# An attention-and-experts layer on one core: stacked operands copied through DRAM instead of within SBUF and by identity products

## The reference, cut to what matters

```
x = x + layernorm(attention(layernorm(x)))
x = x + layernorm(experts(layernorm(x)))

attention:  Q, K, V = x @ w_qkv;  Q_l, K_l = means of 16 tokens of Q, K
            kernel1 = softmax(Q K_l^T); kernel2 = softmax(Q_l K_l^T); kernel3 = softmax(Q_l K^T)
            out = (kernel1 @ iterative_inv(kernel2)) @ (kernel3 @ V) @ w_proj
experts:    loss_e = mean((relu(x Wd1_e) Wd2_e - x)^2);  e = argmin loss
            out = x W_base + relu(x Wa_down_e) Wa_up_e  (+ biases)
```

## Time and profile before

| | |
|---|---|
| median of three runs | 2256.9 us |
| the profiled execution | 2251.81 us |
| its span, first to last instruction | 2250.1 us |
| TensorE busy | 2045.9 us (91% of the span) |
| VectorE busy | 1471.5 us (65%) |
| ScalarE busy | 864.0 us (38%) |
| mean granted TensorE clock | 0.987 of full speed |

### The profile page before, as it was taken

The page is one execution under the profiler, slowest core; times in us unless marked ns, Lnnn a source line. Parts: engine busy times, 40 slices in busy tenths (PEclk is TensorE's granted clock), DMA queues, the critical chain, the costliest instruction groups (busy, mean ns, idle before and its releaser), DMA issues.

```text
span 2250.1 us, 59443 instructions
## 1 busy us (share of the span) xinstructions
PE 2045.9 (91%) x25341; PEld 1321.1 (59%) x25341; DVE 1471.5 (65%) x3319; ACT 864.0 (38%) x1509; POOL 701.1 (31%) x916
## 2 busy tenths in 40 slices
PE   4889999999999999999999999999999999999955
PEld 2655657566574756657475565756657475665724
DVE  4667575776757676675766767576675767767541
ACT  3334344343434434343344434334343443434221
POOL 4153142422315232332523224252231524223052
PEclk9999999999999999999999999999999999999978
DMA  6223151331414122151422315132231513213020
GB/s 156 45 54 71 30 130 33 90 63 42 102 30 124 38 80 65 20 133 30 116 47 70 64 30 132 30 100 53 64 80 30 131 32 88 64 35 92 12 57 19
DMA packets 232974, 150.74 MB, mean 67 GB/s; under 512 B 153035, under 2 KB 203732, under 8 KB 232693
## 3 DMA queue, kind: packets, MB, share of 16 engines
q1 hardware_dynamic: 232710, 146.95, 27.7%
HBM read 36.98 MB, written 16.78 MB: 24 GB/s over the span
## 4 chain that ended last, share of the span: by engine, by line
PE 60%; DVE 18%; SPq 8%; issue 4%; ACT 3%; POOL 3%; DMA 2%; DVEq 1%; POOLq 0%; ACTq 0%
PE NS L986 11%; PE ringF L1194 9%; SPq L429 8%; PE ringF L1179 6%; PE KV L1067 5%; PE ringA L1153 5%; PE ringA L880 4%; DVE mx L1541 3%; PE ringF L1227 3%; DVE stage L1631 3%; PE ringA L1053 3%; PE ringA L1029 3%; PE ringF L880 2%; PE ringF L1229 2%; ACT E L690 2%
## 5 line engine op out<-in xcount | busy, mean ns | idle before, releaser
L1194 PE MATMUL ringF<-x,H 128*128 128x256 f16 x1536 | 237.9, 273 | 0.0
L1555 DVE TENSOR_REDUCE mx<-ringA 128x8 f32<-128x512 f32 x256 | 175.6, 686 | 88.4 <-PE ringA L1029 87.9
L682 ACT ACTIVATE E<-ringA,score_scale 128x512 f32<-128x512 f32 x256 | 175.4, 686 | 116.3 <-PE ringA L1053 115.9
L1194 PE MATMUL ringF<-H 128*128 128x128 f16 x1024 | 204.5, 220 | 1.4 <-DVE H L1642 1.4
L1608 DVE SCALAR_TENSOR_TENSOR X<-X,NS 128x320 f32<-128x320 f32 x160 | 78.1, 488 | 179.0 <-PE NS L986 173.8
L516 POOL TENSOR_SCALAR vtmp<-mv,eps_ffn 128x8 f32<-128x8 f32 x16 | 5.0, 316 | 607.7 <-DVE mv L1386 607.7
L880 PE MATMUL ringA<-xT,wqkv 128*128 128x512 f16 x768 | 176.5, 379 | 16.9 <-ACT QS L700 11.7
L1179 PE MATMUL ringF<-wd,x2T 128*128 128x512 f16 x768 | 185.4, 380 | 3.4 <-DVE H L1642 3.2
L690 ACT ACTIVATE E<-ringA,score_scale 128x512 f32<-128x512 f32 x256 | 158.6, 684 | 73.3 <-PE ringA L1084 73.3
L1541 DVE TENSOR_REDUCE mx<-ringA 128x1 f32<-128x512 f32 x256 | 160.2, 683 | 28.6 <-PE ringA L1020 28.6
L516 POOL TENSOR_SCALAR vtmp<-mv,eps_ln 128x8 f32<-128x8 f32 x32 | 9.9, 310 | 516.2 <-DVE mv L1386 516.2
(11 more groups left out here) (263 smaller groups left out, 4425.5 us busy)
## 6 DMA issues: line engine op xcount, KB each, us to landing
KS<-stage SPq DMA_DIRECT2D x384, 64.0 KB, 2.0
QS<-stage SPq DMA_DIRECT2D x384, 64.0 KB, 2.0
xin<-in_L_attn_x_dram SPq DMA_DIRECT2D x16, 1024.0 KB, 10.9
xres<-in_L_attn_x_dram SPq DMA_DIRECT2D x16, 1024.0 KB, 8.0
out_dram<-yout SPq DMA_DIRECT2D x16, 1024.0 KB, 5.5
QS<-LB SPq DMA_DIRECT2D x16, 512.0 KB, 4.4
E<-in_L_attn_w_qkv_dram SPq DMA_DIRECT2D x1, 768.0 KB, 7.2
H<-in_L_ffn_Wd_dram SPq DMA_DIRECT2D x2, 256.0 KB
```

The costliest lines, as they stand in the source:

```text
L682: A(E[:, k % ESLOTS, :], ps[:, :], ACT.Exp, scale=score_scale[:, 0:1]).then_inc(freed["s3"].sem, 1)
L1194: ins = MM(dst, H[:, a, t, own], src, start=first and i == 0, stop=last and i >= 3, skip_group_check=True)
L1555: V_.reduce_max(mx1[:, t, 8 * h:8 * h + 8], take(b, "m1", k)[:, :].rearrange("p (a m) -> p a m", a=8), AX.X)\
```

## The change

Three parts change.

- **Keys and queries go through DRAM.** For each j one DMA writes both halves of a slot of `stage` (512 KB) to a DRAM tensor `stack_rows`, and three DMAs, one for each group of 32 rows, read them back (256 KB each). A slot is free for ACT when the write has landed. A stack takes 1 + 3 DMAs where it took 12.
- **Landmarks go through DRAM.** Two DMAs write `LB` and `LC` to DRAM; 18 DMAs (six each) read `QlB`, `KlC` and `KlB` back. The 36 identity products on PE, the five copies on ACT and their five uses of `ringA` are gone.
- **Orders change.** SP first writes j = 0, 1 and the landmarks, then reads j = 0, `QlB`, j = 1, `KlC`, `KlB`, then writes j = 2, 3 and reads them, and only then issues the transposes of `x2T` and the fold rows. On PE the third pv comes ahead of m3 0, and the scores of kernel2 go from before m3 0 to after m3 8; seven of eight `keep_warm` products before m3 5 are gone. On ACT the two halves of `x16` (`halves2`) follow pk 6 and 7 together.

```diff
-        stk = [sig(f"stack{j}", 12, 16) for j in range(4)]
+        stk = [sig(f"stack{j}", 3, 16) for j in range(4)]
...
+        scratch = nc.dram_tensor("stack_rows", [4, P, 2, N], F16, kind="Internal").ap()
+        scratch_b = nc.dram_tensor("landmark_rows", [P, 2, 2, 2, P], F16, kind="Internal").ap()
+        scratch_c = nc.dram_tensor("landmark_columns", [P, 2, 2, M], F16, kind="Internal").ap()
...
+            def write_rows(b, js):
+                for j in js:
+                    sp.wait_ge(freed["pk"].sem, freed["pk"].at(b, 2 * j + 2))
+                    sp.sem_inc(s_apart, 1)
+                    sp.dma_start(scratch[j, :, :, :], stage[:, j % 2, :, :]).then_inc(stw[j].sem, 16)
+            def write_landmarks(b):
+                sp.wait_ge(freed["ql"].sem, freed["ql"].at(b, 1))
+                sp.sem_inc(s_apart, 1)
+                sp.dma_start(scratch_b, LB[:, :, :, :, :]).then_inc(lmw.sem, 16)
+                sp.dma_start(scratch_c, LC[:, :, :, :]).then_inc(lmw.sem, 16)
+            def read_landmarks(b, dst, rows, parts, done):
+                sp.wait_ge(lmw.sem, lmw.at(b, 2))
+                sp.sem_inc(s_apart, 1)
+                for a, part in enumerate(parts):
+                    for g in range(2):
+                        ins = sp.dma_start(dst[32 * a:32 * a + 32, 4 * g:4 * g + 4, :],
+                                           rows[:, part, g, :].rearrange("(q r) n -> r q n", r=32))
+                        ins.then_inc(done.sem, 16)
+            def read_rows(b, js):
+                for j in js:
+                    sp.wait_ge(stw[j].sem, stw[j].at(b, 1))
+                    sp.sem_inc(s_apart, 1)
+                    S = KS if j < 2 else QS
+                    for a, part in enumerate((0, 1, 0)):
+                        sp.dma_start(S[32 * a:32 * a + 32, 4 * (j % 2):4 * (j % 2) + 4, :],
+                                     scratch[j, :, part, :].rearrange("(q r) n -> r q n", r=32)).then_inc(stk[j].sem, 16)
...
-                    for q in range(4):
-                        if j == 2 and q == 2 and not first(b):
-                            transposes2(b - 1)
-                        for a, part in enumerate((0, 1, 0)):
-                            sp.dma_start(S[32 * a:32 * a + 32, 4 * (j % 2) + q, :],
-                                         stage[32 * q:32 * q + 32, j % 2, part, :]).then_inc(stk[j].sem, 16)
...
+                write_rows(b, (0, 1))
+                write_landmarks(b)
+                read_rows(b, (0,))
+                read_landmarks(b, QlB, scratch_b[:, 1, :, :, :], (0, 0, 1), stq)
+                read_rows(b, (1,))
+                read_landmarks(b, KlC, scratch_c, (0, 1, 0), stc)
+                read_landmarks(b, KlB, scratch_b[:, 0, :, :, :], (0, 0, 1), stb)
+                write_rows(b, (2, 3))
...
+                read_rows(b, (2, 3))
+                if not first(b):
+                    transposes2(b - 1)
+                fold_rows3(b)
...
                     if j >= 2:
-                        act.wait_ge(stk[j - 2].sem, stk[j - 2].at(b, 12))
+                        act.wait_ge(stw[j - 2].sem, stw[j - 2].at(b, 1))
...
                 if k == 0:
-                    pe.wait_ge(stk[0].sem, stk[0].at(b, 12))
+                    pe.wait_ge(stk[0].sem, stk[0].at(b, 3))
+                    pe.wait_ge(stq.sem, stq.at(b, 6))
...
                     if k == 5:
-                        keep_warm(512, 8)
+                        keep_warm(512, 1)
```

More of the change, by code:

```diff
@@ L173, in sandwich_kernel @@
         USES_A = ([("pk", k) for k in range(4)] + [("kl", 0), ("ql", 0)] + [("pv", k) for k in range(2)]
-                  + [("lk", k) for k in range(3)] + [("lq", k) for k in range(2)] + [("pk", k) for k in (4, 5)]
+                  + [("pk", k) for k in (4, 5)] + [("pv", 2)]
                   + [("m3", k) for k in range(4)] + [("pk", 6), ("m3", 4), ("pk", 7)]
-                  + [("m3", k) for k in range(5, 9)] + [("pv", 2)] + [("m3", k) for k in range(9, 13)] + [("pv", 3)]
+                  + [("m3", k) for k in range(5, 13)] + [("pv", 3)]
                   + [("m3", k) for k in range(13, 16)] + [("f3", 0)])
@@ L240, in sandwich_kernel @@
         pk_hi = sig("pk_hi", 8)
-        stk = [sig(f"stack{j}", 12, 16) for j in range(4)]
+        stk = [sig(f"stack{j}", 3, 16) for j in range(4)]
+        lmw = sig("landmarks_written", 2, 16)
+        stq = sig("stack_ql", 6, 16)
+        stc = sig("stack_klc", 6, 16)
+        stb = sig("stack_klb", 6, 16)
+        stw = [sig(f"stack_written{j}", 1, 16) for j in range(4)]
         l_hi = sig("landmark_hi", 2)
@@ L414, in body @@
                     sp.dma_start(xin[:, :, :], tok(x[b + 1, :, :])).then_inc(x_in.sem, 16)
[L415 to L422, removed]
-                    sp.sem_inc(s_apart, 1)
-                    S = KS if j < 2 else QS
-                    for q in range(4):
-                        if j == 2 and q == 2 and not first(b):
-                            transposes2(b - 1)
-                        for a, part in enumerate((0, 1, 0)):
-                            sp.dma_start(S[32 * a:32 * a + 32, 4 * (j % 2) + q, :],
-                                         stage[32 * q:32 * q + 32, j % 2, part, :]).then_inc(stk[j].sem, 16)
+                write_rows(b, (0, 1))
[7 more added lines that the diff above has]
+                if not first(b):
+                    sp.wait_ge(x1_done.sem, x1_done.at(b - 1, 2))
+                    sp.sem_inc(s_apart, 1)
+                read_rows(b, (2, 3))
+                if not first(b):
+                    transposes2(b - 1)
+                fold_rows3(b)
                 sp.wait_ge(freed["f1"].sem, freed["f1"].at(b, 1))
@@ L644, in landmarks @@
                     ins.then_inc(l_hi.sem, 1)
[L646 to L655, removed]
             def values(b, ks):
@@ L675, in fold_rows1 @@
             def fold_rows1(b):
+                act.wait_ge(lmw.sem, lmw.at(b, 2))
                 A(F1T, take(b, "f1", 0)[0:4 * PAIRS, :].bitcast(F16), ACT.Copy).then_inc(freed["f1"].sem, 1)
@@ L752, in body @@
                 values(b, (0, 1))
-                landmark_stack(b)
                 staged(b, (2,))
-                if ffn:
-                    halves2(b - 1, (0,))
+                values(b, (2,))
                 staged(b, (3,))
                 if ffn:
-                    halves2(b - 1, (1,))
-                values(b, (2, 3))
+                    halves2(b - 1, (0, 1))
+                values(b, (3,))
                 if ffn:
@@ L909, in pool_tokens @@
                 done(ins, "pl")
[L911 to L936, removed]
             def tokens(b, ks):
@@ L970, in project @@
                 values(b, (0, 1))
-                landmark_stacks(b)
             def kernel2_scores(b):
-                pe.wait_ge(freed["lk"].sem, freed["lk"].at(b, 3))
-                pe.wait_ge(freed["lq"].sem, freed["lq"].at(b, 2))
+                pe.wait_ge(stc.sem, stc.at(b, 6))
                 if not first(b):
@@ L1015, in maxima3 @@
                 if k == 0:
-                    pe.wait_ge(stk[0].sem, stk[0].at(b, 12))
+                    pe.wait_ge(stk[0].sem, stk[0].at(b, 3))
+                    pe.wait_ge(stq.sem, stq.at(b, 6))
                 if p == 4:
-                    pe.wait_ge(stk[1].sem, stk[1].at(b, 12))
+                    pe.wait_ge(stk[1].sem, stk[1].at(b, 3))
                 ps = get(b, "m3", k)
@@ L1023, in maxima1 @@
                 h, t = k // T, k % T
+                if k == 0:
+                    pe.wait_ge(stb.sem, stb.at(b, 6))
                 if t == 0:
-                    pe.wait_ge(stk[2 + h].sem, stk[2 + h].at(b, 12))
+                    pe.wait_ge(stk[2 + h].sem, stk[2 + h].at(b, 3))
                 ps = get(b, "m1", k)
@@ L1243, in body @@
                 tokens(b, (4, 5))
-                kernel2_scores(b)
+                values(b, (2,))
                 if not first(b):
@@ L1259, in body @@
                         tokens(b, (7,))
-                    if k in (8, 12):
-                        values(b, (k // 4,))
+                    if k == 8:
+                        kernel2_scores(b)
+                    if k == 12:
+                        values(b, (3,))
                 if ffn_too:
```

## The result

The changed kernel takes 2418.6 us (median of four, 2417.2 to 2421.4) against 2254.4 us of the kernel before beside it: a ratio of 1.0737, 95% interval 1.0714 to 1.0760. It is slower by 164 us. The forecast was 2410 us, 2285 to 2470.

What follows compares the result with a forecast made beforehand. The prediction took SP's issuing of DMAs as the bound. Later transposes cost 8.5 us a turn and the clock 2.0, 157.5 over 15 turns plus 1 for turn 0, on 2251.8: 2410 us, range 2285 to 2470.

Steps and rivals of the forecast that it cites:

- 8.5 + 2.0 = 10.5 us a turn: First expert tile on PE starts 8.5 us late, plus 2.0 for a halved clock; counted for 15 turns.
- SP's issues: Each DMA issue on SP's queue was priced at 0.63 us, with 1.1 us for one hitch.
- SP comes later and does not wait: SP reaches the second writes at 1118.6, after the eighth key tile is ready at 1116.9, so it does not wait.
- The first product: First product of the maxima on PE starts at 1109.6 instead of 1106.05, 3.5 us late, after `QlB` lands.
- The eighth tile: Eighth key tile on PE comes 6.0 us after the maxima's first product; ready for the second writes at 1116.9.
- the clock as 2.0 us behind the transposes: PE's wait before the first expert tile may halve its clock: 3.0 us lost or nothing, taken as 2.0 a turn.
- the clock stays down: Rival: PE runs the maxima's stage at the lower clock too; 14 us a turn, 2462 us; chance 0.13.
- the level fell once after a wait: In the trace before, PE's clock level fell once after a wait, at 2158.7, 4.5 us into it.
- The transposes' landing: Transposes of `x2T` issued at 1126.0 land after 4.6 us plus 0.8 for reads still draining, at 1131.4.
- Turn 0: Turn 0 has no first expert tile; given 1 us for later fold rows.
- ACT's wait for a slot: Sign in the new trace: ACT no longer waits for a slot of `stage`.
- faster: Rival: removing the DVE's wait for the slot decides; 1.5 us a turn gained, 2229 us; chance 0.07.

Runs made afterwards that it cites:

- Run 3: Changed kernel with the six reads of `KlB` moved behind the transposes of `x2T`: 2413.0 us, 1.0722 of the kernel before.
- run 4: Changed kernel with PE's two long waits filled by idle products, 26 before the maxima and 30 before the first expert tile: 2364.7 us, 1.0505 of the kernel before.
- run 1: Changed kernel with the transposes of `x2T` issued ahead of the six query stack reads instead of behind them: 2395.3 us, 1.0645 of the kernel before.
- run 2: Changed kernel with the transposes of `x2T` issued behind three of the six query stack reads: 2359.1 us, 1.0486 of the kernel before.
- run 5: Kernel before with all four stacks through DRAM and the transposes behind the reads; landmarks stay with products and copies: 2358.7 us, 1.0476 of the kernel before.
- run 8: Kernel before with only the key stacks through DRAM and the load of `xin` behind their reads: 2223.3 us, 0.9881 of the kernel before.
- run 9: run 8 with the landmarks through DRAM too, no identity products, and the load of `xin` behind the landmarks' reads: 2277.6 us, 1.0124 of the kernel before.
- run 7: Kernel before with only the key stacks through DRAM; landmarks, query stacks and transposes as before: 2240.8 us, 0.9959 of the kernel before.

## Why the prediction was right, and where its terms were not

**The mechanism held.** The first expert tile waits for transposes that SP issues behind the reads, and everything behind it on PE moves. Forecast 8.5 + 2.0 = 10.5 us a turn. Measured in the ninth turn: 11.1 for the tile, 1.2 for the tiles behind it at the lower clock, and 0.9 won back between there and the turn's end, together 11.4. On average over the turns: 10.0, 1.9 and 0.9 won back, together 10.9.

**The inner terms were off, in both directions, and made up for each other.** That the total came within 9 us is in part luck.

- *SP's issues* were priced at 0.63 and cost 0.46. SP came to the second writes at +19.8, not +22.9. The store's 0.40 was the nearer row, for issues that touch DRAM. Run 3 shows that this term doesn't bind at all: the step "SP comes later and does not wait" failed. SP waits for the eighth key tile, whose write went out at +24.1 where the sum had the tile ready at +21.2. From there a write of 3.0 us, forecast 3.6, and three reads led to the transposes.
- *The first product* was forecast at +13.9 and came at +15.7: the landmarks' writes landed 5.3 us after the last issue, at +9.6, not at +8.6, and the last read of `QlB` took 3.3 us instead of 2.1.
- *The eighth tile* was counted 6.0 us behind the first product, at the pace of rows 4. It took 7.0: the first wait had halved the clock, and the maxima and the seventh tile ahead of it ran slowly. I had the clock as 2.0 us behind the transposes and as nothing ahead of them; run 4 has 2.0 and 1.5 on average. So the rival "the clock stays down" was right that the first wait lowers the clock too, but not in its size (14 us a turn). The prediction's sentence that the level fell once after a wait in the trace before is wrong: it also fell in turn 0 (0.50 in the stretch 94 to 96) and twice more near the end (0.50 in the stretches 2218 to 2220 and 2234 to 2236).
- *The transposes' landing* was 5.4 us in the sum and 9.6 in the ninth turn (on average 8.6). I took 349 GB/s for the reads and kept 210 as a bound; the stretches show 202. Runs 1 and 2 show that the reads ahead are the cause.
- *Turn 0* was given 1 us and lost 4.9.

So in the ninth turn the transposes went out at +28.6 instead of +30.3 and landed 2.6 us later than forecast. Of the signs named, the transposes near +30, the long wait for `x2T` and the clock below 1.00 came; issues of 0.6 us did not, and ACT's wait for a slot only shrank, from 35.3 to 16.5 us in all.

**The parts.** The landmarks' way costs 3.4 us a turn in the changed kernel (run 5) and 3.1 on top of run 8 (run 9), and some 9 us in turn 0 either time. The query stacks' way and the new place of the transposes and fold rows are the larger part: runs 5 and 7 differ by these alone, 2358.7 against 2240.8 us, 7.9 us a turn. Runs 7 and 8 show that the key stacks' way gains, so the rival "faster" named a true gain, but of one part only. What the products and copies taken away are worth was not measured apart; in run 9 it does not make up for the landmarks' way.

What stays open is why the reads run at half the rate of the loads: source, row length and the 32 destination partitions were not varied apart.

## What to carry to other kernels

Fewer DMA issues help only as long as the issuing queue is what is waited for; a way through DRAM replaces issues by round trips, and two of them in a row ahead of an engine with nothing else to do cost more than the issues did. In these runs the transposes, and in run 1 the 32 KB of fold rows, paid for the large reads ahead of them in the queue, so list what stands behind each big read before moving one. One turn of a loop can mislead: compare means over the turns. Take such a change apart: here the key stacks' part, with one load moved from ahead of it, made the kernel 1.2% faster, and the other parts hid that.

## What the runs showed of the hardware

- Reads from DRAM into 32 partitions kept the DMA engines busy (share 1.05) at 202 GB/s in the stretch 1202 to 1204; the load of `xin` and the first writes ran at 393 in the stretch 1174 to 1178.
- Issuing a DMA that touches DRAM took mostly 0.42 to 0.46 us in the new list, plain copies within SBUF about 0.6.
- 32 KB behind six such reads landed after 6.7 us (run 1, the turn shown) instead of 2.1.
- The granted clock fell from 2.4 to 1.2 GHz in both waits of the turn shown: PE was idle from 1179.66, and the stretch 1184 to 1186 has 0.59; it was idle from 1201.42, and the stretch 1204 to 1206 has 0.71.
